# A graph layer with a routed feed-forward layer: a group of 512 nodes in one step or in two

## The chip, the cores and the metric

The kernel runs on one core of one Trainium2 chip. A core has a matrix engine (TensorE, PE in the profile; its weight loads are PEld), a vector engine (VectorE, DVE), a scalar engine (ScalarE, ACT), GpSimd (POOL), a queue engine (SyncE, SP) and 16 DMA engines. Each engine runs its own program; they meet at semaphores. The time is device microseconds (us) of the launch. The kernel before took 2781.99 us, the median of three runs (2778.76 to 2784.24).

## The reference, cut to what matters

```python
# x (12500, 256); 212,500 edges, sorted by dst; all float32
xn  = layernorm(x)
agg = segment_sum(xn[src] * edge_weight[:, None], dst, 12500)
x   = x + agg @ W.T + b
H   = gelu(layernorm(x) @ W1 + b1)               # 12500 x 1024
p   = softmax(H @ Wg + bg); e = argmax(p)        # one of 8 experts for each node
out = x + p[e] * (H @ Wd[e] + bd[e])
```

There is no product over all experts in the kernel: nodes are sorted into lists by their chosen expert and each list is multiplied with its own `Wd[e]`.

## The kernel before, in words

The work has three stages.

*Preamble.* x is normalised and stored as the table `xn_table`; VectorE works out small integer tables from the sorted `dst`, among them `steps_i`, the list of steps.

*Edge stage.* The edges are cut into 104 edge steps of 16 tiles with 128 edges each. For each tile GpSimd issues one indirect DMA (line 403) that gathers 128 rows of `xn_table` into a ring `xring` of three sections, 16 tiles in each; the gathers of step g wait until TensorE is done with step g-3. In `gather_step` TensorE multiplies each tile with a narrow matrix that holds the edge weights (line 515, into `psR`), then runs four matmuls into a bank that nothing reads (line 521), then places the result (line 527); VectorE copies `psR` to `parts` (line 900), adds into `agg` (line 890) and makes the narrow matrix for the next step (lines 847, 857; 857 is the last instruction of an edge step).

The nodes are cut into 25 groups of 512, four blocks of 128 nodes; the last group has 212 real nodes, that is two blocks. As soon as the edges of a group f are all in, a *group step* stands between two edge steps. TensorE and VectorE read its place from `steps_i` and take the same branch. In the group step of f:

- VectorE: `take_sums(f)` copies the sums out of `agg` (929, 930) and clears them; `normalize(f)` waits for the product with W (569), adds x and b and normalises (1003 to 1014). Then come, for the group before, f-1: `rank_choices` (944 to 961), `add_to_lists` (969 to 979) and `second_part`, which copies H to `rows` (1025) and picks the expert (985 to 993; 993 is the last instruction of a group step).
- TensorE: `hidden(f-1)`, that is ranks (548 to 553), eight chunks of H (592) with `messages(f)` (569) after the third, list columns (560), logits (600), transposes of H (614), a fold (621); then the transposes of the normalised group f (578).
- ScalarE: GELU (466), and the copies of the transposed group (461).

So the first group's step has only its own half (`messages(0)`, `transpose_xn2(0)`), and after the loop stands `hidden(24)` by itself, with one more `rank_list` and `extend_list`, since the choices of a group enter the lists one group later.

SyncE stores, for each group, x and the rows of H and logits (row_table, lines 351 and 361), and loads x of the next (356). After the last edge step it loads all `Wd` (379, eight DMAs of 1 MB) and `bd` (381) into the memory where ring and sums were.

*Routed stage.* From the counts of the lists VectorE makes the permutation (lines 1066 to 1093). Then 105 tiles of 128 nodes run: gather rows (420), transpose (648), multiply with `Wd[e]` (658), scale and add, scatter to `out` (428). GpSimd's first gather there waits for the permutation, for `bd`, and for the store of all rows.

Empty places of a tile point to rows behind the real ones, from `PAD_ROW` = 12544 on, one for each of the 128 partitions.

Of the kernel before, what the change touches and what calls it, by code (L numbers as in the profile page):

```python
# [23 lines left out]
P = 128  # L24
# [12 lines left out]
NB = NODES // P  # L37
EDGES = 212500
# [11 lines left out]
STEPS = NG + NF  # L50
# [19 lines left out]
PAD_ROW = N + (-N) % 64  # L70
# [23 lines left out]
def build(nc, x, srcT, dstT, wT, gnn_WT, gnn_b, W1, b1T, Wg, bg, Wd, bd, out):  # L94
    assert PAD_ROW + P <= NODES and NB % LN_ROWS == 0
    ctx = ExitStack()
    with ctx:
# [10 lines left out]
        row_dram = nc.dram_tensor("row_table", (NODES, ROW), F32, kind="Internal").ap()  # L108
# [28 lines left out]
        steps_i = sb("steps_i", [P, STEPS, 6], I32)  # L137
# [65 lines left out]
        u = [selv[:, a * STEPS:(a + 1) * STEPS] for a in range(7)]  # L203
# [118 lines left out]
        def _(sp):  # L322
# [25 lines left out]
            def store_x2(f):  # L348

                sp.wait_ge(s_xn2, f + 1)  # L350
                sp.dma_start(row_dram[bass.ds(f * GROUP, GROUP), 0:C].rearrange("(q p) c -> p q c", p=P),
                             xg[:, :, :]).then_inc(s_x2_st, 16)
                sp.wait_ge(s_x2_st, f * 16 + 16)

            def load_x(f):
                sp.dma_start(xg[:, :, :], x[bass.ds(f * GROUP, GROUP), :]
                             .rearrange("(q p) c -> p q c", p=P)).then_inc(s_xg, 16)

            def store_rows(f):
                sp.wait_ge(s_rows, f + 1)  # L360
                sp.dma_start(row_dram[bass.ds(f * GROUP, GROUP), C:ROW].rearrange("(q p) c -> p q c", p=P),
                             rows[:, :, C:ROW]).then_inc(s_rows_st, 16)
# [19 lines left out]
            store_rows(NF - 1)  # L382
# [65 lines left out]
        def _(act):  # L448
# [9 lines left out]
            def copy_xn2T(f):  # L458
                for k in range(KC):
                    act.wait_ge(s_xt, f * KC + k + 1)  # L460
                    nc.scalar.activation(xn2T[:, k, :], psH[k][:, :], ACT.Identity).then_inc(s_xtc, 1)

            def hidden(f):
                for c in range(HC):
                    act.wait_ge(s_h, f * HC + c + 1)
                    nc.scalar.activation(hidT[:, c, :], psH[c % 2][:, :], ACT.Gelu,  # L466
                                         bias=b1[:, c:c + 1]).then_inc(s_gelu, 1)
                act.wait_ge(s_gp, f + 1)
                nc.scalar.activation(gate_parts[:, :], psG[:, :], ACT.Identity).then_inc(s_gc, 1)

            copy_xn2T(0)
            with act.Fori(0, NF - 1) as f:
                hidden(f)
                copy_xn2T(f + 1)
            hidden(NF - 1)


# [17 lines left out]
        def _(pe):  # L495
# [23 lines left out]

# [23 lines left out]
            def rank_list(b):  # L543
# [4 lines left out]
                nc.tensor.matmul(psE[0][:, at], upper[:, :], oh, start=True, stop=False)  # L548
                for d in range(1, QB):
                    nc.tensor.matmul(psE[0][:, at.start + d * E:at.stop], ones[:, :], oh[:, 0:(QB - d) * E],  # L550
                                     start=False, stop=(d == QB - 1))
                for q in range(QB):
                    mm = nc.tensor.matmul(psE[0][:, total], ones[:, :], oh[:, q * E:(q + 1) * E],
                                          start=(q == 0), stop=(q == QB - 1))
                mm.then_inc(s_rank, 1)

            def extend_list(b):
                pe.wait_ge(s_rank_oh, b + 1)
                for q in range(QB):
                    mm = nc.tensor.matmul(psE[0][:, list_new], slot_oh[:, q, :], col_oh[:, q, :],  # L560
                                          start=(q == 0), stop=(q == QB - 1))
                mm.then_inc(s_list, 1)

            def messages(f):

                pe.wait_ge(s_aggs, f + 1)
                for q in range(QB):
# [6 lines left out]
            def transpose_xn2(f):  # L574
                pe.wait_ge(s_xn2, f + 1)
                for k in range(KC):
                    for q in range(QB):
                        mm = nc.tensor.transpose(psH[k][:, q * P:(q + 1) * P],
                                                 xn2[:, q, k * P:(k + 1) * P], ident[:, :])
                    mm.then_inc(s_xt, 1)  # L580

            def hidden(f, following=None):
                rank_list(f)
                pe.wait_ge(s_xtc, f * KC + KC)
                for c in range(HC):
                    if c == 3 and following is not None:
                        messages(following)
# [3 lines left out]
                    for k in range(KC):  # L591
                        mm = nc.tensor.matmul(psH[c % 2][:, :], w1[:, k, c * P:(c + 1) * P], xn2T[:, k, :],  # L592
# [5 lines left out]
                for c in range(HC):  # L598
                    cg = c % 4
                    mm = nc.tensor.matmul(psG[cg * GATE_COLS:(cg + 1) * GATE_COLS, :], wg[:, c, :], hidT[:, c, :],  # L600
                                          start=(c < 4), stop=(c >= 4))
                mm.then_inc(s_gp, 1)
                if following is not None:

                    pe.wait_ge(s_xn2, f + 2)
                else:

                    pe.wait_ge(s_ev, f * (2 * QB))
                for i in range(2 * QB):
                    half, q = i // QB, i % QB  # L610
# [9 lines left out]
                for q in range(QB):  # L620
# [4 lines left out]
            with pe.Fori(0, STEPS) as k:  # L625
# [11 lines left out]
            hidden(NF - 1)  # L637


            rank_list(NF)  # L640
            extend_list(NF)
# [34 lines left out]
        def _(dve):  # L676
# [94 lines left out]
            for a, span in enumerate((span_tile, span_oct)):  # L771
# [3 lines left out]
            tick(nc.vector.tensor_scalar(stats[:, 0, 0:1], part[:, :], float(GROUP), float(GROUP),  # L775
                                         ALU.mult, ALU.add))
# [400 lines left out]
```

## Time and profile before

| | |
|---|---|
| median of the three runs | 2781.99 us |
| the profiled execution's own time | 2780.53 us |
| its span, first to last instruction | 2778.4 us |
| busy: PE, PEld, DVE, ACT, POOL | 1877.3, 1192.6, 1079.9, 444.4, 1842.4 us |
| mean granted TensorE clock | 0.851 of full speed |

The profile gives each group of instructions with its line, engine, operation, the tile written and the tiles read, the count, the busy time and the mean duration, then the idle time of the engine just before them and what ended it. "issue" means that the engine waited for nothing that the profile shows. In a timeline a row is: start in us, duration in us, engine, line, operation, and in brackets the idle time before it with its releaser. A table by windows has, for each stretch: its length, the busy time of PE, PEld, DVE, ACT and POOL with the instruction counts, the granted clock (1 is 2.4 GHz), the DMA engines' busy share and the GB/s. Spans of POOL are rough. A matmul of 32-bit floats appears as two rows.

### The profile page before, as it was taken

The numbers are of one execution on the slowest core, as the hardware profiler recorded it, in microseconds if no ns is written. First come the engines' busy times: TensorE is split into PE (matmuls) and PEld (weight loads), VectorE is DVE, ScalarE is ACT, GpSimd is POOL, SyncE is SP. The second block draws the span as 40 slices with busy tenths as digits, with TensorE's granted clock in tenths as the row PEclk, the third lists the DMA queues.
The fourth block names the chain that finished last, engine by engine and source line by source line (L and its number), as shares of the span: only waits on it lengthen the run. The fifth ranks groups of instructions, "written<-read, shape, count | busy, mean of one in ns | idle before, by whom it ended". The sixth has DMA issues, their size and how long they took to land.

```text
span 2778.4 us, 39308 instructions
## 1 busy us (share of the span) xinstructions
PE 1877.3 (68%) x10522; PEld 1192.6 (43%) x10523; DVE 1079.9 (39%) x3491; ACT 444.4 (16%) x847; POOL 1842.4 (66%) x1988
## 2 busy tenths in 40 slices
PE   0235675666756667666667566675667777999998
PEld 0122343333433333333334233343333446888887
DVE  8522443334433344343444234443344453333332
ACT  7000110100101001010011000110001113333332
POOL 0677777777777777777777777777777403555553
PEclk9966887888878789788888788887888888999999
DMA  9434444444444444444444344443444354555554
GB/s 396 150 103 119 149 148 120 134 148 147 149 117 132 149 149 148 119 135 147 148 149 149 104 148 149 148 149 111 141 149 149 108 204 152 182 181 179 182 179 128
DMA packets 153598, 420.31 MB, mean 151 GB/s; under 512 B 33320, under 2 KB 67499, under 8 KB 150880
## 3 DMA queue, kind: packets, MB, share of 16 engines
q0 software_dynamic: 100032, 300.27, 36.7%
q1 hardware_dynamic: 53536, 119.73, 11.7%
q14 instruction: 23, 0.19, 0.0%
q8 instruction: 7, 0.11, 0.0%
HBM read 328.02 MB, written 92.82 MB: 151 GB/s over the span
## 4 chain that ended last, share of the span: by engine, by line
POOL 45%; PE 27%; issue 18%; DVE 5%; DMA 2%; DVEq 1%; SPq 0%; POOLq 0%
POOL big L403 45%; PE psA L658 3%; PE psH L658 3%; PE psG L658 3%; PE psE L658 3%; PE psH L592 2%; PE psR L515 2%; PE psA L614 1%; PE psG L600 1%; PE psA L569 1%; DMA src_i<-in_srcT 1%; PE psH L648 1%; PE psE L521 1%; PE psA L648 1%; PE psE L648 1%
## 5 line engine op out<-in xcount | busy, mean ns | idle before, releaser
L403 POOL DMA_INDIRECT big<-xn_table,src_i x1664 | 1610.6, 968 | 581.5 <-issue 579.3
L515 PE MATMUL psR<-big,sel_narrow 128*32 128x256 f32 x3328 | 297.6, 519 | 597.7 <-DMA big<-xn_table,src_i 409.8
L515 PEld LDWEIGHTS psR<-big,sel_narrow 128*32 128x32 f32 x3328 | 127.1, 141 | 715.0 <-issue 630.6
L466 ACT ACTIVATE hidT<-psH,b 128x512 f32<-128x512 f32 x200 | 137.4, 687 | 1506.5 <-PE psH L592 1506.5
L592 PE MATMUL psH<-xn2T,w 128*128 128x512 f32 x800 | 374.4, 624 | 0.0
L900 DVE COPY parts<-psR 128x512 f32<-128x512 f32 x104 | 71.5, 687 | 439.0 <-PE psR L515 438.9
L521 PE MATMUL psE<-w,ident 128*128 128x512 f32 x416 | 240.8, 707 | 0.0
L592 PEld LDWEIGHTS psH<-xn2T,w 128*128 128x128 f32 x800 | 157.8, 200 | 182.6 <-issue 181.3
L894 DVE TENSOR_TENSOR place<-iota,shift_f 128x160 f32<-128x160 f32 x104 | 34.5, 332 | 328.8 <-issue 328.8
L420 POOL DMA_INDIRECT rows<-row_table,stage x105 | 104.1, 991 | 86.8 <-POOL stage L417 86.8
L417 POOL COPY stage<-rel_f 128x1 int32 (+1 forms) x105 | 19.2, 183 | 213.4 <-DVEq L1098 107.2
L1025 DVE COPY rows<-psA 128x512 f32<-128x512 f32 x200 | 128.9, 686 | 40.5 <-PE psA L614 35.9
L527 PEld LDWEIGHTS psE<-place,parts 128*128 128x128 f32 x832 | 107.7, 191 | 84.1 <-DVE parts L900 51.4
L521 PEld LDWEIGHTS psE<-w,ident 128*128 128x128 f32 x416 | 87.0, 234 | 131.8 <-issue 131.8
L890 DVE TENSOR_TENSOR big<-psE,big 128x160 f32 x208 | 67.5, 325 | 185.0 <-PE psE L527 170.2
L428 POOL DMA_INDIRECT out<-big,st_out x105 | 107.3, 1022 | 43.6 <-issue 30.4
L614 PE MATMUL psA<-ident,hidT 128*128 128x128 f32 x800 | 122.6, 287 | 18.4 <-DVE rows L1025 18.4
L527 PE MATMUL psE<-place,parts 128*128 128x80 f32 x832 | 107.1, 272 | 27.6 <-DVE parts L900 27.6
L614 PEld LDWEIGHTS psA<-ident,hidT 128*128 128x128 f32 x800 | 85.3, 142 | 86.9 <-DVE rows L1025 49.7
L560 PE MATMUL psE<-col_oh,big 128*128 128x40 f32 x208 | 38.6, 347 | 95.2 <-DVE big L961 95.2
L658 PE MATMUL psA<-big,hidT 128*128 x432 | 98.7, 382 | 0.0
L569 PE MATMUL psA<-wt,aggs 128*128 128x256 f32 x400 | 92.8, 386 | 6.6 <-DVE aggs L930 6.6
(207 smaller groups left out, 2415.2 us busy)
## 6 DMA issues: line engine op xcount, KB each, us to landing
row_table<-rows SPq DMA_DIRECT2D x25, 2064.0 KB, 8.0
big<-xn_table,src_i POOLq DMA_INDIRECT x1664
big<-in_x SPq DMA_DIRECT2D x10, 1280.0 KB, 17.4
xn_table<-big SPq DMA_DIRECT2D x10, 1280.0 KB, 13.2
big<-in_x SPq DMA_DIRECT2D x25, 512.0 KB
row_table<-big SPq DMA_DIRECT2D x25, 512.0 KB, 3.9
big<-in_Wd SPq DMA_DIRECT2D x8, 1024.0 KB, 12.7
hidT<-in_dstT SPq DMA_DIRECT2D x2, 840.0 KB, 30.5
```

The costliest lines, as they stand in the source:

```text
L403: nc.gpsimd.indirect_dma_start(out=xring[:, h * STEP_TILES + j, :], out_offset=None, in_=xn_dram[:, :], in_offset=bass.IndirectOffsetOnAxi ...
L420: nc.gpsimd.indirect_dma_start(out=grow[i], out_offset=None, in_=row_dram[:, :], in_offset=bass.IndirectOffsetOnAxis(ap=st_in[:, i:i + 1], ...
L428: nc.gpsimd.indirect_dma_start(out=out[:, :], out_offset=bass.IndirectOffsetOnAxis(ap=st_out[:, i:i + 1], axis=0), in_=ybuf[i], in_offset= ...
L466: nc.scalar.activation(hidT[:, c, :], psH[c % 2][:, :], ACT.Gelu, bias=b1[:, c:c + 1]).then_inc(s_gelu, 1)
L515: mm = nc.tensor.matmul(psQ[j * LANES:(j + 1) * LANES, o * C:(o + 1) * C], sel_narrow[:, t, :], xring[:, t, :], start=(odd == 0), stop=(od ...
L521: nc.tensor.matmul(psW[:, :], ident[:, :], w1[:, 0, 0:512], start=True, stop=True)
L527: mm = nc.tensor.matmul(psW[:, at:at + SPAN], parts[:, o, k * P:(k + 1) * P], place[:, o, :], start=True, stop=True)
L569: mm = nc.tensor.matmul(psA[q // 2][:, (q % 2) * C:(q % 2 + 1) * C], aggs[:, k, q * P:(q + 1) * P], wt[:, k, :], start=(k == 0), stop=(k = ...
L592: mm = nc.tensor.matmul(psH[c % 2][:, :], w1[:, k, c * P:(c + 1) * P], xn2T[:, k, :], start=(k == 0), stop=(k == KC - 1))
L614: mm = nc.tensor.transpose(psA[i % 2][:, j * P:(j + 1) * P], hidT[:, 4 * half + j, q * P:(q + 1) * P], ident[:, :])
L658: mm = nc.tensor.matmul(psY2[i], hT2[i][:, c, :], wd[:, bass.ds(e8 + c, 1), :], start=(c == 0), stop=(c == HC - 1))
L1025: nc.vector.tensor_copy(rows[:, q, C + half * 512:C + (half + 1) * 512], psA[i % 2][:, :]).then_inc(s_ev, 1)
```

## The change

The group step is cut in two. The first (kind `SECTIONS`) has `take_sums(f)`, `messages(f)` and `normalize(f)`, and stands where the group step stood. The second (kind `SECTIONS + 1`) has `layers(f)`: transposes, ranks, the chunks of H and all that followed, now for the same group f; it stands one edge step later, or together with the first step of the next group if that comes sooner. The list of steps has 104 + 48 entries; the 25th group is no longer in it, but written out behind the loop for two blocks instead of four. `hidden(24)` for four blocks is gone. Empty places now point to 32 rows from 12500 on, four partitions to a row.

On SyncE the store of the last group's x, which stood ahead of the loads of `Wd` and `bd`, comes behind them.

```diff
-STEPS = NG + NF
+STEPS = NG + 2 * (NF - 1)
+LAST_QB = -(-(N - (NF - 1) * GROUP) // P)          # 2
-PAD_ROW = N + (-N) % 64
+PAD_LANES = 32
...
 @ SyncE
-            store_x2(0)
-            load_x(1)
             with sp.Fori(0, NF - 2) as f:
-                store_x2(f + 1)
-                load_x(f + 2)
+                store_x2(f)
+                load_x(f + 1)
                 store_rows(f)
-            store_x2(NF - 1)
+            store_x2(NF - 2)
+            load_x(NF - 1, LAST_QB)
             store_rows(NF - 2)
...
             sp.dma_start(bd_bc, ...)
-            store_rows(NF - 1)
+            store_x2(NF - 1, LAST_QB)
+            store_rows(NF - 1, LAST_QB)
...
 @ TensorE
-            def transpose_xn2(f):
+            def layers(f, blocks=QB):
+                cols = blocks * P
                 pe.wait_ge(s_xn2, f + 1)
...                                                  # transposes of xn2
-            def hidden(f, following=None):
                 rank_list(f)
                 pe.wait_ge(s_xtc, f * KC + KC)
                 for c in range(HC):
-                    if c == 3 and following is not None:
-                        messages(following)
...
                 mm.then_inc(s_gp, 1)
-                if following is not None:
-                    pe.wait_ge(s_xn2, f + 2)
-                else:
-                    pe.wait_ge(s_ev, f * (2 * QB))
-                for i in range(2 * QB):
+                for i in range(2 * blocks):
...
                 with pe.If(kind == SECTIONS):
-                    before = n.with_bounds(min_val=0, max_val=NF - 2)
-                    hidden(before, before + 1)
-                    transpose_xn2(before + 1)
+                    messages(n.with_bounds(min_val=0, max_val=NF - 2))
                 with pe.If(kind == SECTIONS + 1):
-                    messages(0)
-                    transpose_xn2(0)
-            hidden(NF - 1)
-            rank_list(NF)
-            extend_list(NF)
+                    layers(n.with_bounds(min_val=0, max_val=NF - 2))
+            messages(NF - 1, LAST_QB)
+            layers(NF - 1, LAST_QB)
+            rank_list(NF, LAST_QB)
+            extend_list(NF, LAST_QB)
...
 @ VectorE, the list of steps: partition 2f is the first step of group f, 2f + 1 its second
+            nc.vector.tensor_scalar(second_i, part_i[:, :], 1, None, ALU.bitwise_and)
+            tick(nc.vector.tensor_scalar(group_i, part_i[:, :], 1, None, ALU.logical_shift_right))
...
+            tick(nc.vector.tensor_tensor(second_i, steps_of[:, 0:1], second_i, ALU.add))
+            tick(nc.vector.tensor_tensor(second_i, second_i, steps_of[:, 1:2], ALU.min))
+            tick(nc.vector.tensor_tensor(stats[:, 4, 0:1], second_i, part[:, :], ALU.add))
...
-                with dve.If(kind >= SECTIONS):
+                with dve.If(kind == SECTIONS):
...
                     take_sums(link, f, g, slot, spill)
                     normalize(link, f)
-                with dve.If(kind == SECTIONS):
+                with dve.If(kind == SECTIONS + 1):
...
-                    rank_choices(tie, before)
-                    add_to_lists(tie, before)
-                    second_part(tie, before)
+                    rank_choices(tie, f)
+                    add_to_lists(tie, f)
+                    second_part(tie, f)
...
-            rank_choices(tie, NF - 1)
-            add_to_lists(tie, NF - 1)
-            second_part(tie, NF - 1)
-            rank_choices(tie, NF)
+            take_sums(link, last, NG, last % NS * SLOT, (last - 1) % NS * SLOT + GROUP, LAST_QB)
+            normalize(link, last, LAST_QB)
+            rank_choices(tie, last)
+            add_to_lists(tie, last)
+            second_part(tie, last, LAST_QB)
+            rank_choices(tie, NF, LAST_QB)
             add_to_lists(tie, NF)
```

ScalarE's program follows: for each group the two copies, eight GELUs and one copy of the logits, and two blocks' width for the last.

How the program order moves, as the instructions stand. TensorE, the group step in the loop, before (`psA<-wt,aggs` is `messages`, `psH<-xn2T,w` a chunk of H, `psE<-col_oh,big` the list columns, `psG` the logits, `psA<-ident,hidT` the transposes of H, `psH<-ident,big` those of the normalised group):

```order
L548 MATMUL psE<-chosen,upper 128x32
...
L592 MATMUL psH<-xn2T,w 128x512 x4
L590 ISA
L592 MATMUL psH<-xn2T,w 128x512 x2
L566 REGISTER_ALU
L569 MATMUL psA<-wt,aggs 128x256 x8
...
L560 MATMUL psE<-col_oh,big 128x40 x4
L596 REGISTER_ALU
L600 MATMUL psG<-hidT,wg 32x512 x8
L614 MATMUL psA<-ident,hidT 128x128 x32
L621 MATMUL psE<-fold,big 128x8 x4
L578 MATMUL psH<-ident,big 128x128 x8
```

TensorE, the two group steps in the loop, after the change:

```order
L618 COMPARE_AND_BRANCH
L562 REGISTER_ALU
L565 MATMUL psA<-wt,aggs 128x256 x8
L618 UNCONDITIONAL_BRANCH
L620 COMPARE_AND_BRANCH
L572 REGISTER_ALU
L575 MATMUL psH<-ident,big 128x128 x8
L544 MATMUL psE<-chosen,upper 128x32
...
L557 MATMUL psE<-col_oh,big 128x40 x4
L590 REGISTER_ALU
L594 MATMUL psG<-hidT,wg 32x512 x8
L602 MATMUL psA<-ident,hidT 128x128 x32
```

`messages` has left the chunks of H and stands alone in a branch of its own; the transposes of the normalised group have moved from the end of the step to the start of the second one.

SyncE from the last turn of its loop to the end, before (`row_table<-big` stores x, `row_table<-rows` stores H and logits):

```order
L351 DMA row_table<-big 128x4x256
L361 DMA row_table<-rows 128x4x1032
L379 DMA big<-in_Wd 128x8x256 x8
L381 DMA big<-in_bd 128x2048
L361 DMA row_table<-rows 128x4x1032
```

SyncE from the last turn of its loop to the end, after the change:

```order
L355 DMA row_table<-big 128x4x256
L359 DMA big<-in_x 128x2x256
L363 DMA row_table<-rows 128x4x1032
L379 DMA big<-in_Wd 128x8x256 x8
L381 DMA big<-in_bd 128x2048
L355 DMA row_table<-big 128x2x256
L363 DMA row_table<-rows 128x2x1032
```

Two stores, each of half the width, now stand behind the nine loads where one store of full width stood; the second waits for the first to land.

## Rows read from the trace of the kernel before

**Rows 1.** Table by windows: the end of the edge stage, the routed stage.
```profile
2194.10:2301.30 107.20, 76.90 (x392) 45.67 (x392) 53.06 (x198) 16.92 (x24) 0.00 (x0) 0.85 0.46 155
2301.30:2778.40 477.10, 457.69 (x2520) 408.29 (x2520) 139.99 (x525) 180.36 (x445) 230.52 (x315) 0.98 0.55 172
```

**Rows 2.** Costliest groups and timeline of POOL: all gathers, the first and the last.
```profile
L403 POOL DMA_INDIRECT big<-xn_table,src_i x1664 | 1610.6, 968 | 581.5 <-issue 579.3
...
76.88 1.16 POOL L403 DMA_INDIRECT big<-xn_table,src_i  x1 [74.90 <-issue]
...
2193.12 0.95 POOL L403 DMA_INDIRECT big<-xn_table,src_i  x1 [0.30 <-issue]
```

**Rows 3.** Timeline around one group step, steps 97 to 99; POOL's section 101.
```profile
2074.26 3.64 PE L515 MATMUL psR<-big,sel_narrow 128*32 128x256 f32 x32 [11.62 <-DMA big<-xn_table,src_i]
...
2091.24 3.62 PE L569 MATMUL psA<-wt,aggs 128*128 128x256 f32 x16
...
2119.53 0.19 DVE L993 TENSOR_TENSOR chosen<-route_b,valid 128x32 f32<-128x32 f32 x1
...
2120.98 2.38 PE L515 MATMUL psR<-big,sel_narrow 128*32 128x256 f32 x32 [2.13 <-issue]
...
2132.72 0.95 POOL L403 DMA_INDIRECT big<-xn_table,src_i  x1 [0.30 <-issue]
...
2145.36 0.68 DVE L857 TENSOR_TENSOR sel_narrow<-sel_narrow,w_f  x1
```

**Rows 4.** Timeline of the first group's step, which has no `hidden`.
```profile
182.67 3.64 PE L515 MATMUL psR<-big,sel_narrow 128*32 128x256 f32 x32 [13.70 <-DMA big<-xn_table,src_i]
...
190.36 0.68 DVE L857 TENSOR_TENSOR sel_narrow<-sel_narrow,w_f  x1
194.67 0.72 DVE L929 COPY aggs<-big 128x1024 f32 x1 [3.62 <-issue]
...
196.01 5.98 PE L569 MATMUL psA<-wt,aggs 128*128 128x256 f32 x16 [6.59 <-DVE aggs L930]
...
209.89 1.46 DVE L1014 TENSOR_SCALAR big<-big,meanvar,rstd 128x256 f32<-128x256 f32 x4
...
211.40 1.97 PE L578 MATMUL psH<-ident,big 128*128 128x128 f32 x8 [9.41 <-DVE big L1014]
...
214.02 0.33 DVE L894 TENSOR_TENSOR place<-iota,shift_f 128x160 f32<-128x160 f32 x1 [2.67 <-issue]
```

**Rows 5.** Timeline of `hidden(24)`, which runs alone behind the loop.
```profile
2252.92 0.41 PE L548 MATMUL psE<-chosen,upper 128*128 128x32 f32 x2 [0.93 <-DVE chosen L993]
...
2254.73 15.68 PE L592 MATMUL psH<-xn2T,w 128*128 128x512 f32 x32
...
2281.39 0.19 DVE L993 TENSOR_TENSOR chosen<-route_b,valid 128x32 f32<-128x32 f32 x1
```

**Rows 6.** Timeline: ends of edge steps 101 and 103, start of the routed stage.
```profile
2163.28 0.68 DVE L857 TENSOR_TENSOR sel_narrow<-sel_narrow,w_f  x1
...
2217.46 0.68 DVE L857 TENSOR_TENSOR sel_narrow<-sel_narrow,w_f  x1
...
2301.30 0.18 POOL L417 COPY stage<-rel_f 128x1 int32<-128x1 int32 x1 [107.23 <-DVEq L1098]
```

**Rows 7.** SyncE's timeline at the end of the edge stage; landing times of lines 361, 381.
```profile
2258.26 19.20 SPq L379 DMA_DIRECT2D big<-in_Wd  x8
...
2280.37 0.80 SPq L361 DMA_DIRECT2D row_table<-rows  x1
...
DMA to landing us min/median/max: 6.6/10.2/13.8
...
DMA to landing us min/median/max: 11.5/11.5/11.5
```

**Rows 8.** TensorE's first edge step (timeline); the scan for the list of steps (groups by shape).
```profile
107.64 3.64 PE L515 MATMUL psR<-big,sel_narrow 128*32 128x256 f32 x32 [26.79 <-issue]
...
L778 DVE TENSOR_SCALAR_CACHE_REDUCE rows<-rows,stats 128x1664 f32<-128x1664 f32 x1 | 1.9, 1947 | 0.0
```

More of the change, by code:

```diff
@@ L202, in build @@
         span_tile, span_oct = (xn2T[:, a, 0:NG] for a in range(2))
-        u = [selv[:, a * STEPS:(a + 1) * STEPS] for a in range(7)]
+        u = [selv[:, a * STEPS:(a + 1) * STEPS] for a in range(9)]
         small = xn2T[:, :, :].rearrange("p a b -> p (a b)")
@@ L572, in messages @@
                 mm.then_inc(s_z, 1)
-            def transpose_xn2(f):
+            def layers(f, blocks=QB):
+                cols = blocks * P
                 pe.wait_ge(s_xn2, f + 1)
                 for k in range(KC):
-                    for q in range(QB):
+                    for q in range(blocks):
                         mm = nc.tensor.transpose(psH[k][:, q * P:(q + 1) * P],
@@ L618, in hidden @@
                 pe.wait_ge(s_listed, f + 1)
-                for q in range(QB):
+                for q in range(blocks):
                     mm = nc.tensor.matmul(psE[0][:, q * E:(q + 1) * E], gate_parts[:, q * P:(q + 1) * P],
@@ L817, in _ @@
             is_group, groups, gathers, section, prev = (a.bitcast(I32) for a in (u[2], u[3], u[4], u[5], u[0]))
-            nc.vector.tensor_scalar(prev, groups, float(NS - 1), None, ALU.add)
+            slots, earlier, second, group_of = (u[a].bitcast(I32) for a in (1, 6, 7, 8))
+            nc.vector.tensor_scalar(second, groups, 1, None, ALU.bitwise_and)
+            nc.vector.tensor_scalar(group_of, groups, 1, None, ALU.logical_shift_right)
             tick(nc.vector.tensor_tensor(gathers, iota_i[:, 0:STEPS], groups, ALU.subtract))
+            nc.vector.tensor_scalar(prev, group_of, float(NS - 1), None, ALU.add)
+            nc.vector.tensor_scalar(slots, group_of, NS - 1, None, ALU.bitwise_and)
+            nc.vector.tensor_tensor(second, second, is_group, ALU.mult)
+            nc.vector.tensor_tensor(earlier, gathers, group_of, ALU.subtract)
+            tick(nc.vector.tensor_scalar(section, gathers, 171.0, None, ALU.mult))
             nc.vector.tensor_scalar(prev, prev, NS - 1, None, ALU.bitwise_and)
-            tick(nc.vector.tensor_scalar(section, gathers, 171.0, None, ALU.mult))
+            nc.vector.tensor_tensor(earlier, earlier, is_group, ALU.mult)
             tick(nc.vector.tensor_scalar(section, section, 9, None, ALU.logical_shift_right))
@@ L1016, in normalize, with second_part @@
                 o.then_inc(s_xn2, 1)
-            def second_part(tie, f):
+            def second_part(tie, f, blocks=QB):
                 dve.wait_ge(s_rows_free, f + 1)
                 dve.sem_inc(s_pass_dve, 1)
-                for i in range(2 * QB):
-                    half, q = i // QB, i % QB
+                for i in range(2 * blocks):
+                    half, q = i // blocks, i % blocks
                     dve.wait_ge(s_tr, f * (2 * QB) + i + 1)
```

202 lines of the change are left out of this document (98 added, 104 removed).

## The prediction

> **What bounds the kernel now.** I read the page first: POOL 1842 us busy, PE 1877, neither full, so the stages have different limits. The table by windows cuts it: 107 us lie between the last gather and the first routed one, with POOL at 0.00, and the routed stage of 477 us has PE busy for 458 [rows 1]. Then POOL's groups and timeline: 1664 gathers, 968 ns each, and 581.5 us idle, of which 74.9 stand ahead of the first. That leaves 506.6 over 1663 gaps, 0.30 us each: the gap between any two gathers, so GpSimd never waits for a free section. From 76.88 to 2194.07 (2193.12 + 0.95) it takes 2117.2 us, or 20.36 per edge step [rows 2]. The edge stage is POOL's, and work of TensorE and VectorE in it counts only if it lasts so long that the ring runs full. The chain of waits passes through group steps in the edge stage, but POOL's own rows show no wait there; I go by the rows.
>
> How near is the ring to full? In the step shown, TensorE starts step 97 on its data at 2074.26, and step 98 only at 2120.98, after the group step, 26 us behind its data. It is done at 2123.36; POOL needs that section at 2132.72: 9.4 us to spare [rows 3].
>
> So the change can win at the end of the edge stage, and it can lose by starving POOL.
>
> **The edge stage, part by part.** The first step of a group is in the trace already: the first group's step has only that half. From the end of line 857 (191.04) to the end of line 1014 (211.35) it takes 20.3 us: 3.6 until line 929, then `messages`, which waits for the sums and takes 5.98, then the normalisation [rows 4]. In the usual group step `messages` takes 3.62 [rows 3], under the chunks of H. So this step costs 17.9 to 20.3. I take 20.3: its place in the program is that of rows 4, with TensorE idle for 6.59 ahead of it.
>
> The edge step between the two halves: VectorE is at line 894 2.67 us after the normalisation [rows 4], and TensorE has done its matmuls while VectorE normalised. Three edge steps in a row without data to wait for take 26.3 us (2119.72 to 2146.04), 8.8 each; the matmuls in one of them are 2.38 [rows 3]. I take 2.0 off: 6.8, with 5.9 and 8.8 as ends.
>
> The second half: `hidden(24)` alone took 28.66 from its ranks to the choice (2252.92 to 2281.58) [rows 5]. Ahead of it now come the transposes, 1.97 after a wait [rows 4]. If TensorE enters when line 857 ends, that makes 30.6; TensorE's last part of an edge step ends somewhat before line 857, and with transposes at twice the rate (1.0) and chunks without a slow start (14.0 instead of 15.68) it would be about 27.5. TensorE has waited for VectorE before it, so I take 29.5, nearer to the slow end. The list columns need no normalisation any more and follow H at once, as in `hidden(24)`.
>
> A cycle with four edge steps is then 20.3 + 6.8 + 29.5 + 26.3 = 82.9 us against POOL's 81.4 (4 x 20.36). With five it is 91.7 against 101.8. From the starts of line 929 (25, the first in [rows 4]) 18 intervals have four steps and 5 have five, and at most five fours stand in a row. So the two engines fall behind by 1.5 us per four, 7.5 at worst, and a five clears it. The spare time, from TensorE's start of step s: VectorE ends the step 8.4 later (182.67 to 191.04) [rows 4], then 20.3 + 6.8 + 29.5, and the matmuls of s+2 are done 3.6 after that (2119.72 to 2123.36): 68.6. POOL started section 101 58.5 after TensorE's start of step 97 [rows 3]; it wants the section of s+2 one edge step later in the same count, at 78.8. So 10.2 to spare, more than 7.5: no stall, and the edge stage ends where it did. This is the cover for all that the first half costs, and it is nearly used up.
>
> Unknown here is whether GpSimd's gathers change beside another order of the same VectorE instructions: nothing is added, so I take zero; if a gather took 1% more or less it would be 21 us either way, which I hold unlikely.
>
> The preamble gets some ten small instructions and a second scan of 1.95 us. TensorE's first edge step stood at 107.64 [rows 8]; POOL's first wait for it comes three sections after 76.88, at 138: covered, with 26 us over.
>
> **The end of the edge stage.** Before, line 857 of step 101 ended at 2163.96 and of step 103 at 2218.14; the permutation was out at 2301.30, 83.2 us after it [rows 6]. Between lay a half-hidden group step and `hidden(24)` for four blocks.
>
> After: 2163.96, 4.5 late (three fours), + 20.3 + 6.8 + 29.5 + 8.8 for step 103 = 2233.9, that is 15.8 later than before, since group 23 is now worked off there. Then the last group in two blocks:
> - sums, messages, normalisation: 20.3, less 2.6 for half of `messages` at the slow rate and 2.9 for half of the wide VectorE instructions (lines 929 and 1014 of [rows 4] give 0.3 and 0.7 of that): 14.8.
> - transposes, half of 1.97, and ranks, 2.7: 3.7.
> - the chunks, half of 15.68, and 0.7 for a slow start: 8.5.
> - logits to choice: 11.2 in `hidden(24)` (2270.41 to 2281.58) [rows 5], with half of its eight copies gone: 7.7.
> - from the choice to the permutation 19.7 (2281.58 to 2301.30), less 2.3 for shorter ranks, columns and one-hots: 17.4.
>
> Sum 52.1, so 2286.0 in place of 2301.3: 15.3 us earlier. The routed stage is as it was: the same 105 tiles.
>
> On SyncE the last group's stores stand behind the weights. The weights' loads wait for the sums to be cleared, at about 2239; issuing them took 19.2 and `bd` lands 11.5 after its issue [rows 7], so at about 2270. The x store lands just behind, and the rows of two blocks some 6 later (a full store took 6.6 by itself and 13.8 behind the loads [rows 7]): 2277, before 2286. Nine us of cover; if it went, GpSimd's first routed gather would wait for that store.
>
> TensorE's clock is the price inside these numbers: `messages` took 5.98 after a pause and 3.62 without one, and the stretch at the end of the edge stage shows a granted clock of 0.85 against 0.98 in the routed stage [rows 1, 3, 4]; full is 2.4 GHz, the other level 1.2. The Trainium skill, "TensorE: Matmul & The Clock Gate", section "HAM oscillation — how this bites in real kernels", speaks against this change: a loop whose matmul bursts are parted by waits re-enters the slow rate in each turn, and should be laid out so that they stay together. By that rule, carried to the whole second half, its 14 us of chunks would double. The trace shows only the start slow: 15.68 for 32 rows after a wait. I go by the trace.
>
> **Rivals.**
> 1. *POOL starves.* The cycle is longer than reckoned: a slow second half, or hand-overs I don't see. For: only 1.5 us per four are assumed, and a few us of slow clock in each group are enough. Against: the spare 10.2 and the fives. At 84.5 per four POOL would lose some 5 us and the end come 5 later: near 2776. From 85 on it is slower than before; at 86, 4.6 per four and 7 given back per five make 18 x 4.6 - 5 x 7 = 48, less 10 to spare: 38 lost, 8 more at the end, 15 won: 2782 + 31 = 2813.
> 2. *The stores end last.* The x store waits longer behind 9 MB, and the rows behind it. For: the serial wait is new. Against: nine us of cover. With 8 to 15 us more the gain shrinks to 15 or to 9: 2767 to 2773.
> 3. *Everything runs at the fast rate*, and no lateness builds up: 17.9 and 27.5 instead of 20.3 and 29.5, lateness 0, and 3 less in the last group: 15.3 + 2.4 + 2 + 4.5 + 3 = 27 earlier: 2755.
> 4. *The second half stands right behind the first*, if the list of steps makes it so: then it is 49.8 in one piece, 12 more than before, and the ring runs full in most groups: past 2790. By the diff it can't, save where two groups meet: chance 1 in 100.
>
> **How the numbers follow.** The sum was made on the profiled execution, 2780.5; the median of the runs, 2782, lies 1.5 above. 2782 - 15.3 = 2766.7, so 2766. Chances: forecast 0.60 (2759 to 2774 of its own), rival 1 0.19 (of it 0.12 slower than before by over 0.2%, 0.05 within, 0.02 faster), rival 2 0.08 (0.02 within), rival 3 0.12, rival 4 0.01. A difference of 0.2%, 5.6 us, is about what can be told from none. The forecast leaves 0.04 within that. So faster 0.76, same 0.11, slower 0.13. The range 2752 to 2788 leaves out the far end of rival 1 and little of rival 3.
>
> **What would show it.** Right: POOL's idle in front of line 403 still about 581; `messages` near 6 us; a cycle of 82 to 84; the first routed copy on POOL about 15 earlier, released by VectorE. Wrong: gaps of POOL over 0.4 us released by `psR`, or a first routed gather released by a store.

## The result, and the profile after

The changed kernel took 2793.70 us, the median of seven runs (2791.47 to 2796.10); the kernel before, run beside it, 2785.03 (2778.76 to 2786.32). The ratio is 1.0031, 95% interval 1.0021 to 1.0041: slower by some 9 us, where 2766 was forecast. The profiled execution took 2791.47 us with a span of 2789.5.

I read the page's groups and GpSimd's timeline of after first, to compare with [rows 2]. Columns as there: count, busy, mean ns, idle time; in the timeline start, duration, and in brackets the idle time before.

```profile
L404 POOL DMA_INDIRECT big<-xn_table,src_i x1664 | 1613.6, 970 | 597.1 <-issue 578.3
...
775.54 0.94 POOL L404 DMA_INDIRECT big<-xn_table,src_i  x1 [4.08 <-PE psR L512]
...
1472.87 0.94 POOL L404 DMA_INDIRECT big<-xn_table,src_i  x1 [5.08 <-PE psR L512]
...
1906.31 0.95 POOL L404 DMA_INDIRECT big<-xn_table,src_i  x1 [5.04 <-PE psR L512]
...
2211.72 0.94 POOL L404 DMA_INDIRECT big<-xn_table,src_i  x1 [0.30 <-issue]
...
2311.36 0.18 POOL L418 COPY stage<-rel_f 128x1 int32<-128x1 int32 x1 [98.70 <-DVEq L1093]
```

The idle time is 15.6 us more than the 581.5 before. It sits in five gaps that end with a matmul into `psR`: the three above, and two more of 1.25 and 1.53. GpSimd waited for a free section of the ring. The gathers themselves are busy for 3.0 us more (1613.6 against 1610.6; why is not shown, and in the runs below this sum lies anywhere between 1602.1 and 1616.8), so the last one ends at 2212.7 instead of 2194.1: 18.6 later. The first routed copy is 10.1 later than the 2301.30 of [rows 6], released by VectorE, and the routed stage takes 1.0 longer. These make the 11 us between the profiled executions.

Why the ring ran full is seen in one usual group (timelines of TensorE and VectorE in after; line 846 ends an edge step, as 857 did before):

```profile
1151.56 0.68 DVE L846 TENSOR_TENSOR sel_narrow<-sel_narrow,w_f  x1
...
1156.70 6.18 PE L565 MATMUL psA<-wt,aggs 128*128 128x256 f32 x16 [6.20 <-DVE aggs L919]
...
1170.76 1.45 DVE L1003 TENSOR_SCALAR big<-big,meanvar,rstd 128x256 f32<-128x256 f32 x4
...
1175.88 2.00 PE L523 MATMUL psE<-place,parts 128*128 128x80 f32 x8 [4.89 <-DVE parts L889]
1178.94 0.68 DVE L846 TENSOR_TENSOR sel_narrow<-sel_narrow,w_f  x1
1179.94 1.96 PE L575 MATMUL psH<-ident,big 128*128 128x128 f32 x8 [2.06 <-issue]
1181.69 0.47 PE L544 MATMUL psE<-chosen,upper 128*128 128x32 f32 x2
...
1184.97 15.98 PE L586 MATMUL psH<-xn2T,w 128*128 128x512 f32 x32
...
1212.15 0.19 DVE L982 TENSOR_TENSOR chosen<-route_b,valid 128x32 f32<-128x32 f32 x1
```

The first half goes from 1152.24 to 1172.21: 20.0 us (20.3 forecast). The edge step between takes 7.4, to 1179.62 (6.8). The second half takes 32.7, to 1212.34 (29.5). Over the 24 groups of the loop the second half has a mean of 32.7 (32.3 to 32.9): it is the same everywhere.

The table by windows of the same stretch (length; busy us of PE, PEld, DVE, ACT, POOL with counts; granted clock; DMA share; GB/s) shows the clock:

```profile
1170.00:1174.00 4.00, 0.99 (x3) 0.16 (x1) 2.07 (x8) 0.00 (x0) 3.05 (x4) 1.00 0.38 110
1174.00:1180.00 6.00, 2.06 (x9) 1.85 (x10) 2.77 (x6) 0.00 (x0) 4.51 (x5) 0.61 0.87 274
1180.00:1185.00 5.00, 5.00 (x25) 5.00 (x25) 0.00 (x0) 2.48 (x3) 3.78 (x5) 0.50 0.33 102
1185.00:1201.00 16.00, 16.00 (x36) 7.14 (x36) 2.92 (x15) 4.82 (x8) 12.04 (x14) 0.87 0.35 104
```

TensorE does little from 1170 to 1180 (3.05 us of 10), while VectorE normalises and does its part of the edge step. Its transposes and ranks then take 5.0 us, all of them at a granted clock of 0.50, that is 1.2 GHz, and the chunks begin there too. In `hidden(24)` of before the ranks took 1.8 [rows 5], at 1.00, as its window in the kernel before shows:

```profile
2252.90:2254.73 1.83, 1.81 (x16) 1.81 (x17) 0.00 (x0) 0.00 (x0) 0.00 (x0) 1.00 1.02 408
```

With this the distance from one group's sums to the next (starts of the copy in `take_sums`, 18 intervals with four edge steps) has a mean of 85.2 us (84.2 to 86.4), against 81.6 before, where GpSimd sets it, and 82.9 in the forecast.

At the end of the edge stage (timelines of VectorE and SyncE in after), for [rows 6] and [rows 7]:

```profile
2192.90 0.68 DVE L846 TENSOR_TENSOR sel_narrow<-sel_narrow,w_f  x1
...
2261.25 0.68 DVE L846 TENSOR_TENSOR sel_narrow<-sel_narrow,w_f  x1
...
2263.74 17.81 SPq L379 DMA_DIRECT2D big<-in_Wd  x8
...
2295.20 0.38 SPq L363 DMA_DIRECT2D row_table<-rows  x1
```

Step 101 ends at 2193.6, 25.1 later than the 2168.5 of the forecast; from there to the end of step 103 it takes 68.35 (65.4 forecast); and from that end to the first routed copy 49.4 us, where it was 83.2 before.

### The profile page after: what moved, and what is told of

It is laid out like the page before. It is cut to its first block and busy times, and to the rows that moved or that the text cites. A ratio compares the mean times of both kernels' runs of the same rounds, so it can differ in the third digit from the quotient of the medians.

```text
span 2789.5 us, 39686 instructions
## 1 busy us (share of the span) xinstructions
PE 1942.8 (70%) x10478; PEld 1288.8 (46%) x10479; DVE 1076.4 (39%) x3487; ACT 475.1 (17%) x871; POOL 1845.3 (66%) x1988
## 3 DMA queue, kind: packets, MB, share of 16 engines
q1 hardware_dynamic: 52768, 118.15, 11.7%
## 5 line engine op out<-in xcount | busy, mean ns | idle before, releaser
L404 POOL DMA_INDIRECT big<-xn_table,src_i x1664 | 1613.6, 970 | 597.1 <-issue 578.3
L512 PE MATMUL psR<-big,sel_narrow 128*32 128x256 f32 x3328 | 270.0, 479 | 256.0 <-issue 127.9
L586 PE MATMUL psH<-xn2T,w 128*128 128x512 f32 (+1 forms) x800 | 393.4, 656 | 0.0
L462 ACT ACTIVATE xn2T<-psH 128x512 f32<-128x512 f32 (+1 forms) x50 | 29.4, 588 | 1605.6 <-PE psH L575 1605.6
L523 PE MATMUL psE<-place,parts 128*128 128x80 f32 x832 | 131.5, 310 | 232.9 <-DVE parts L889 232.7
L586 PEld LDWEIGHTS psH<-xn2T,w 128*128 128x128 f32 x800 | 171.8, 219 | 202.9 <-issue 201.2
L523 PEld LDWEIGHTS psE<-place,parts 128*128 128x128 f32 x832 | 124.7, 223 | 299.5 <-DVE parts L889 280.3
L565 PE MATMUL psA<-wt,aggs 128*128 128x256 f32 x392 | 151.0, 567 | 151.1 <-DVE aggs L919 151.1
L517 PE MATMUL psE<-w,ident 128*128 128x512 f32 x416 | 222.5, 659 | 0.0
L565 PEld LDWEIGHTS psA<-wt,aggs 128*128 128x128 f32 x392 | 114.6, 300 | 180.8 <-DVE aggs L919 154.9
L466 ACT ACTIVATE hidT<-psH,b 128x512 f32<-128x512 f32 (+1 forms) x200 | 135.7, 678 | 305.4 <-PE psH L586 305.4
L602 PE MATMUL psA<-ident,hidT 128*128 128x128 f32 x784 | 118.9, 285 | 32.9 <-DVE rows L1014 32.9
```

Source lines behind the costliest of these rows:

```text
L404: nc.gpsimd.indirect_dma_start(out=xring[:, h * STEP_TILES + j, :], out_offset=None, in_=xn_dram[:, :], in_offset=bass.IndirectOffsetOnAxi ...
L466: nc.scalar.activation(hidT[:, c, 0:blocks * P], psH[c % 2][:, 0:blocks * P], ACT.Gelu, bias=b1[:, c:c + 1]).then_inc(s_gelu, 1)
L512: mm = nc.tensor.matmul(psQ[j * LANES:(j + 1) * LANES, o * C:(o + 1) * C], sel_narrow[:, t, :], xring[:, t, :], start=(odd == 0), stop=(od ...
L517: nc.tensor.matmul(psW[:, :], ident[:, :], w1[:, 0, 0:512], start=True, stop=True)
L523: mm = nc.tensor.matmul(psW[:, at:at + SPAN], parts[:, o, k * P:(k + 1) * P], place[:, o, :], start=True, stop=True)
L565: mm = nc.tensor.matmul(psA[q // 2][:, (q % 2) * C:(q % 2 + 1) * C], aggs[:, k, q * P:(q + 1) * P], wt[:, k, :], start=(k == 0), stop=(k = ...
```

## The experiments

Nine kernels were run, each timed beside the kernel before. The theory at the start: the loop loses, because TensorE comes to the second half at the lower clock, the cycle grows past GpSimd's 81.4 us and the ring runs full; the last group wins. The rivals: two blocks are worth little; the place of the second half hurts, and not its length.

| label | edit | median us | ratio to before, 95% |
|---|---|---|---|
| e1_tail_only | loop of before, last group of two blocks | 2768.28 | 0.9947 (0.9934 to 0.9961) |
| e2_last_four | after, last group of four blocks | 2811.30 | 1.0106 (1.0091 to 1.0122) |
| e3_warm | after, 8 matmuls behind `messages` | 2791.89 | 1.0035 (1.0021 to 1.0049) |
| e3b_warm_eleven | the same with 11 | 2790.11 | 1.0009 (0.9999 to 1.0019) |
| e4_two_steps | after, second half two edge steps behind the first | 2765.49 | 0.9940 (0.9926 to 0.9953) |
| e7_two_steps_longer | e4, second half 4.4 us longer | 2857.87 | 1.0246 (1.0228 to 1.0264) |
| e0_right_behind | after, no edge step between | 2885.73 | 1.0361 (1.0343 to 1.0379) |
| e8_shorter_half | after, second half shorter: five of its chunk matmuls are left out | 2757.55 | 0.9916 (0.9901 to 0.9931) |
| e6_two_steps_overlap | e4, group 23 and the last group overlapped | 2754.65 | 0.9881 (0.9864 to 0.9897) |

**The two parts apart.** e1_tail_only keeps the group step of before in the loop:

```diff
-                    messages(n.with_bounds(min_val=0, max_val=NF - 2))
+                    before = n.with_bounds(min_val=0, max_val=NF - 3)
+                    hidden(before, before + 1)
+                    transpose_xn2(before + 1)
...
-            messages(NF - 1, LAST_QB)
-            layers(NF - 1, LAST_QB)
+            hidden(NF - 2, NF - 1, QB, LAST_QB)
+            transpose_xn2(NF - 1, LAST_QB)
+            hidden(NF - 1, None, LAST_QB)
```

> The group steps inside the loop are those of before (one step per group: chunks of H of the group before, with the messages of the next after the third); only the last group is written out behind the loop for two blocks instead of four. My theory: all that the change loses it loses inside the loop, by the cycle of 86 us, and all that it wins it wins in the last group. Then GpSimd shows no gap over 0.4 us, its last gather starts at about 2194 as before, and the permutation is out 10 to 14 us earlier than the 2301.3 of before: 2772 to 2776 against 2785. Rival (the two blocks are worth little, since the chain behind the choice is as long as before): within 4 us of before, 2781 to 2789.

It took 2768.28, 13.3 below the 2781.61 of before beside it, where 9 to 13 were expected. The page and GpSimd's and SyncE's timelines of this kernel:

```profile
L404 POOL DMA_INDIRECT big<-xn_table,src_i x1664 | 1610.6, 968 | 581.6 <-issue 579.5
...
2252.06 18.53 SPq L380 DMA_DIRECT2D big<-in_Wd  x8
...
2273.51 0.80 SPq L363 DMA_DIRECT2D row_table<-rows  x1
...
2284.98 0.18 POOL L418 COPY stage<-rel_f 128x1 int32<-128x1 int32 x1 [90.79 <-SPq L365]
```

No stall, and the permutation out at 2281.3 (end of VectorE's last line, 1106), 20 earlier than the 2301.3 of before. But the copy waits 3.6 us more for the store of rows, which stands behind 9 MB of weights: rival 2 of the prediction, in another kernel than the one that it was meant for. So the two blocks win and the loop loses.

e2_last_four takes the two blocks away:

```diff
-LAST_QB = -(-(N - (NF - 1) * GROUP) // P)
+LAST_QB = QB
```

> After, with the last group written out for four blocks instead of two. My theory: the loop is as in after (stalls of 15 us on GpSimd, last gather at 2212), and only the last group is longer, by half of its chunks (8), half of the eight copies (3.5), half of the wide steps (5) and shorter ranks and columns: 10 to 18 us over after, 2804 to 2812. Rival (the gain came from where the halves stand, not from the two blocks): under 5 us over after.

2811.30, as expected. Its first routed copy starts at 2332.15, 68.2 us after step 103 ended (2263.94); in after it was 49.4. Two blocks in place of four are worth 18.8 us.

**The clock, tried directly.** e3_warm and e3b_warm_eleven:

```diff
                     messages(n.with_bounds(min_val=0, max_val=NF - 2))
+                    for _ in range(8):                       # 11 in the second
+                        nc.tensor.matmul(psW[:, :], ident[:, :], w1[:, 0, 0:512], start=True, stop=True)
```

> After, with eight more matmuls of 128x512 into the bank that nothing reads, behind the messages in the first half of each group, where TensorE waits for the normalisation. My theory: the second half is 32.6 us in place of 29.5 because TensorE comes to the transposes and ranks at the granted clock 0.50; busy through the pause it keeps the upper level, ranks fall from 5.1 to about 2 us, the second half to 28.6 to 30, the cycle from 86 to 82 to 83.5: GpSimd's stalls fall from 15.6 to under 4 us, line 846 of step 103 ends 20 to 30 us earlier, and the time is 2760 to 2775. Rival (the second half is long for what VectorE does in it, the clock is a bystander): ranks get shorter but the cycle stays at 85 to 87, and the time is 2788 to 2800, as in after or longer by the added work.

> As the run with eight added matmuls, but with eleven. Eight left TensorE idle for 2.4 us ahead of the place matmuls, and the transposes and ranks still ran at the granted clock 0.50; eleven last until the place matmuls can start. Theory A (the second half is too long, for its clock): granted clock 1.00 in transposes and ranks, second half 28 to 29 us in place of 32.6, no gap of GpSimd over 0.4 us, the choice of group 23 at about 2231, time 2758 to 2770. Theory B (one edge step between the halves is too little for the ring, whatever the second half takes): ranks get faster, but gaps of GpSimd released by the matmuls of psR stay, 8 us or more in sum, and the time is 2780 or more. If the clock stays at 0.50 the run tells nothing of either.

Both missed: 2791.89 and 2790.11, and GpSimd stalled for 17 and 24 us. They don't speak against the theory, since they didn't do what they were made for. The windows of e3b_warm_eleven in one group:

```profile
649.80:653.60 3.80, 3.80 (x37) 1.82 (x30) 1.52 (x3) 0.00 (x0) 2.89 (x4) 1.00 0.77 226
653.60:658.60 5.00, 2.32 (x14) 2.17 (x13) 1.25 (x3) 0.60 (x1) 3.78 (x5) 0.76 0.68 224
658.60:664.00 5.40, 5.40 (x20) 4.37 (x20) 1.63 (x11) 1.88 (x2) 3.88 (x6) 0.50 0.35 98
```

TensorE works without a pause until 654, at 1.00. Then it pauses for 2.68 us until the branch into the second half has its first transpose, and the clock falls to 0.50 while TensorE is busy again. The pause ahead of the transposes is 2.7 to 3.2 us in all 24 groups; in after it is 1.8 to 2.3. In 18 of the 24 groups the transposes took 2.0 us, as in after; in the other six the slow stretch came a little later, in the chunks (16.6 to 16.9 us). The mean second half is 33.4, no shorter than in after.

**Two edge steps between the halves.**

```diff
+            tick(nc.vector.tensor_scalar(second_i, second_i, 2.0, None, ALU.mult))
             tick(nc.vector.tensor_tensor(second_i, steps_of[:, 0:1], second_i, ALU.add))
```

> After, with the second half two edge steps behind the first in place of one. My theory: what starves GpSimd is first the length of the cycle, which is the same sum of parts here (19.9 + 2 x 7.4 + 32.6 + 2 edge steps), a little shorter or equal, and only then where the two halves stand in it: stalls of 3 to 12 us in place of 15.6, last group's place one edge step closer to the end, so 2784 to 2795. Rival (the ring runs full because two halves stand too close, and the length of the cycle is innocent): no stall at all, last gather at 2195, time 2770 to 2780.

2765.49: my theory's number fell. The rival's "no stall at all" came true, with a time still below its 2770 to 2780. GpSimd's idle time is that of before (page of e4_two_steps), and the first routed copy starts at 2286.11. But the second half itself had changed. Page, timelines of TensorE and VectorE, and then the windows of e4_two_steps:

```profile
L404 POOL DMA_INDIRECT big<-xn_table,src_i x1664 | 1607.2, 966 | 581.5 <-issue 578.5
...
232.91 1.09 PE L575 MATMUL psH<-ident,big 128*128 128x128 f32 x8 [2.32 <-issue]
...
236.36 16.52 PE L586 MATMUL psH<-xn2T,w 128*128 128x512 f32 x32
...
635.46 1.93 PE L512 MATMUL psR<-big,sel_narrow 128*32 128x256 f32 x32
...
652.20 3.64 PE L512 MATMUL psR<-big,sel_narrow 128*32 128x256 f32 x32 [1.68 <-DVE sel_narrow L847]
...
660.60 0.68 DVE L847 TENSOR_TENSOR sel_narrow<-sel_narrow,w_f  x1
660.97 1.09 PE L575 MATMUL psH<-ident,big 128*128 128x128 f32 x8 [1.32 <-issue]
661.90 0.31 PE L544 MATMUL psE<-chosen,upper 128*128 128x32 f32 x2
...
663.60 13.98 PE L586 MATMUL psH<-xn2T,w 128*128 128x512 f32 x32
...
688.85 0.19 DVE L983 TENSOR_TENSOR chosen<-route_b,valid 128x32 f32<-128x32 f32 x1
```

```profile
648.00:652.00 4.00, 1.99 (x8) 1.78 (x8) 2.17 (x5) 0.00 (x0) 2.91 (x4) 0.50 0.83 240
652.00:656.00 4.00, 3.80 (x33) 1.61 (x34) 0.56 (x3) 0.00 (x0) 3.09 (x4) 0.50 0.44 137
656.00:661.00 5.00, 3.68 (x13) 2.02 (x13) 2.17 (x5) 0.00 (x0) 3.78 (x5) 0.81 0.37 105
661.00:664.00 3.00, 3.00 (x25) 2.88 (x26) 0.40 (x2) 2.32 (x3) 2.39 (x3) 1.00 0.32 87
664.00:678.00 14.00, 14.00 (x38) 6.47 (x37) 2.64 (x15) 5.24 (x9) 10.65 (x12) 1.00 0.37 106
```

The same instructions take 27.8 us (661.28 to 689.04) in place of 32.7: transposes and ranks 2.6 instead of 5.0, chunks 14.0 instead of 16.0. The second edge step keeps TensorE busy just ahead of them, it is that step that runs at 0.50, and the transposes start at 1.00. The transposes take 1.1 us in all 24 groups; in 15 the whole second half runs fast (27.1 to 27.8), in nine a slow stretch still falls into ranks and chunks (29.6 to 32.0; the chunks from 236.36 are one); the mean is 28.9. The two sorts differ in the pause of TensorE just ahead of the transposes: 0.8 to 1.4 us in the 15, 1.6 to 2.4 in the nine. That is read from rows; no run sets this pause by itself, and what makes it long or short is not shown.

The distance between groups had not become short everywhere. The 18 intervals with four steps have a mean of 84.8, nearly the 85.2 of after. But the first of the loop and the first behind each interval with five steps take 84.5 to 92.4, since TensorE waits for data there again; of the other twelve eight take 82.1 to 82.5. And those with five steps take 90.3 where after has 93.8: against GpSimd's 101.8 each gives back 11.5 us and not 8.0. So in e4 the lateness (counted from the first group against 20.36 us for each edge step) is gone after every interval with five steps, while in after it has grown to 28 us by the last one with four.

So this run changed place and length at once, and can't decide between them. Three more could.

**Length and place apart.** e7_two_steps_longer keeps the place of e4 and gives the length back; e8_shorter_half keeps the place of after and takes the length away; e0_right_behind goes to the other side.

```diff
 e7
                 rank_list(f)
+                for _ in range(5):
+                    nc.tensor.matmul(psG[:, :], ident[:, :], w1[:, 0, 0:512], start=True, stop=True)
 e8
-                    for k in range(KC):
+                    used = 1 if blocks == QB and c < 5 else KC
+                    for k in range(used):
 e0
+            tick(nc.vector.tensor_scalar(second_i, second_i, 0.0, None, ALU.mult))
```

> As the run with the second half two edge steps behind the first, with five more matmuls of 128x512 behind the ranks in every second half (into the bank of the logits, which is free then): the second half is 32.4 us instead of 28.0, as long as in after, but two edge steps away. Theory A (length): the cycle is 87 to 88 us, lateness piles up over the runs of four-step groups; GpSimd may still stall only 1 to 6 us, since two steps give more room, but the choice of group 23 comes at about 2256 instead of 2234.8, and the time is 2784 to 2796. Theory B (place): no stall, group 23 only some 5 to 9 us later, time 2770 to 2778.

> After, one edge step between the halves as there, but in the 24 groups of the loop the first five of the eight chunks of H multiply only half of the input columns: five matmuls of 128x512 fewer, so H, and with it the choices and the output, are other numbers; the lists and the routed stage have the same number of tiles. Adding eight and eleven matmuls to the first half did not raise the clock in the transposes and ranks, so this takes 4.3 us or more (five at 0.86, more where they ran at the lower level) out of the second half in another way: 32.6 becomes 27 to 28.4, as long as with two edge steps between (28.0), and the place stays. Theory A (length): no gap of GpSimd over 0.4 us, or one or two of under 2, last gather at 2190 to 2196, four-step cycles of 81 to 82.5 us where they were 85.2, time 2755 to 2770. Theory B (place, one edge step is too little): four or more gaps released by psR, 8 us or more in sum, time 2778 or more.

> After, with the second half right behind the first, no edge step between. The cycle has the same parts as in after, less the pause between (some 2 us shorter if anything), but the ring must last through both halves at once, 52 us. If the place of the halves counts as well as the length: GpSimd stalls in most groups, 60 to 90 us in sum, time 2835 to 2870. If only the length of the cycle counts: stalls of 0 to 16 us and a time of 2780 to 2795.

The gathers of the three (page; e7, e8, e0 in this order):

```profile
L404 POOL DMA_INDIRECT big<-xn_table,src_i x1664 | 1609.2, 967 | 652.7 <-issue 575.4
```

```profile
L404 POOL DMA_INDIRECT big<-xn_table,src_i x1664 | 1610.5, 968 | 581.6 <-issue 580.7
```

```profile
L404 POOL DMA_INDIRECT big<-xn_table,src_i x1664 | 1615.1, 971 | 697.3 <-issue 575.5
```

e8: second half 28.7 on the mean, cycle 81.3, no stall, 2757.55. One edge step between the halves is enough if the second half is short, and it got short here with its transposes and ranks still at 5.0 us: it is the length that counts, however it comes about. e7: second half 33.4, cycle 88.3, 15 stalls with 70.7 us in sum, 2857.87. Two steps don't help if it is long. So at either place the length decides whether GpSimd stalls (one step between: 15.6 us at 32.7, none at 28.7; two steps: 70.7 at 33.4, none at 28.9), and the rival, that more room between the halves mends it, is refuted.

The place has a price of its own all the same, and it goes the other way: at nearly the same length e7 has a cycle 3.1 longer than after, and only 0.6 of that lies in the second half. The rest is not taken apart; a likely part of it is the clock of the edge step ahead of the second half: its 32 matmuls into `psR` take 3.2 to 3.6 us in all 24 groups of e4 and e7 (0.50 at 652.20 in e4), and 1.9 in 23 of the 24 of after (1.00 at 635.46 in e4).

My number for e7 was far off (2784 to 2796), though the cycle was put nearly right (87 to 88). I had let the lateness pile up and yet given GpSimd only 1 to 6 us of stalls. 18 x 6.9 late less 5 x 6.5 given back (its intervals with five steps take 95.3) is some 92 us; 70.7 of them came out as stalls.

e0 shows that place counts too, beyond a point: the cycle of 86.5 is not far from that of after, yet it has 23 stalls with 115 us. Both halves in one piece last 53.0 us, so the ring runs full in nearly every group, and even intervals with five edge steps take 107 us, where GpSimd needs 101.8: nothing is made good there. It was slower than I expected (2835 to 2870).

**A version that beats both.** e6_two_steps_overlap takes e4 and writes out the second half of group 23 with the last group's first half inside:

```diff
-            messages(NF - 1, LAST_QB)
+            layers(NF - 2, QB, NF - 1, LAST_QB)      # messages(24) after the third chunk
             layers(NF - 1, LAST_QB)
 @ SyncE: loads of Wd and bd, store of the last x, and only then
+            store_rows(NF - 2)
             store_rows(NF - 1, LAST_QB)
```

> A version that should beat both kernels: the second half two edge steps behind the first; the second half of group 23 is taken out of the loop and holds the sums, messages and normalisation of the last group after its third chunk, as the group step of before did; the store of rows of group 23 comes behind the loads of the weights. The serial first half of the last group (2234.8 to 2246.4) goes beside the chunks: 9 to 12 us less than the run with two steps alone, 2753 to 2757. Rival: the stores of rows, now behind the weights, end last, and GpSimd's first routed copy is released by SyncE: 2760 to 2768.

2754.65, ratio 0.9881, as expected. GpSimd's timeline:

```profile
2273.47 0.19 POOL L418 COPY stage<-rel_f 128x1 int32<-128x1 int32 x1 [80.73 <-DVEq L1101]
```

12.6 us earlier than in e4, and released by VectorE, not by a store: the weights are asked for at 2208.5 here, and the last store behind them has landed at 2258.5.

## Why the prediction was wrong

- *What bounds the kernel* was right: GpSimd's gathers set the edge stage as long as TensorE and VectorE make good in the intervals with five steps what they lose in those with four (e8 and e4, no stall in either).
- *The first half*, 20.3: measured 20.0. Right.
- *The edge step between*, 6.8: measured 7.4, inside the bounds of 5.9 and 8.8.
- *The second half*, 29.5: this is the step that failed. It was put between 27.5 and 30.6, and measured 32.7. The slow end took `hidden(24)` as it stood in [rows 5], with ranks of 1.8 us and only a slow start of the chunks. But there TensorE had waited only 0.93 us for the choice, straight behind a group step, and its ranks ran at 1.00. In after it comes from a first half and an edge step in which it waits for VectorE nearly all the time. The row that showed this price was in my own group: transposes 1.97 after a wait of 9.41 [rows 4]. I had counted that slow rate for the transposes and not carried it through the ranks that follow without a pause (1181.69 to 1184.97, 3.3 us instead of 1.8). Of the 3.2 us, 1.5 lie there and 1.1 in my choice of 29.5 below the slow end; the rest is in small steps.
- *The cycle*, 82.9: measured 85.2. Of the excess of 2.3 the second half gives +3.2, the step between +0.6, and the other three edge steps -1.2 or so (25.1, what is left of 85.2, in place of 26.3), with -0.3 from the first half.
- *No stall*: wrong through the cycle alone. Rival 1 had it: "From 85 on it is slower than before", per four steps. With 85.2 in its arithmetic, 18 x 3.8 less 5 x 7.8 given back less 10 to spare makes 19 us of stalls; 15.6 were measured. The forecast's own arithmetic stood as well: e8, with a second half of 28.7, had no stall and took 2757.55.
- *The last group*, 52.1: measured 49.4. The sum is near, in part by luck: sums, messages and normalisation took 9.7 in place of 14.8 (line 918 copies the sums at 2261.85, without the 3.6 us of idle time ahead of it that the row of the loop has), and all behind them 39.7 in place of 37.3.
- *SyncE's stores*: covered, as forecast: the last one, issued at 2295.20, landed 4.5 us later, 11.7 ahead of the copy. In e1 they were uncovered, since the loads of the weights begin 33.8 us after the end of step 103 there (2218.27 to 2252.06), in after 1.8.
- *The sign*: the last group and what lies behind it are 33.7 us shorter (83.2 to 49.4), and the end of step 103 comes 43.8 later. Of these 43.8 the forecast had 15.8, since group 23 is worked off there. The other 28.0 are lateness at step 101 (25.1) and the longer group of 23 (2.9).

The Trainium skill, "TensorE: Matmul & The Clock Gate", section "HAM oscillation — how this bites in real kernels", was the rule that I weighed and set aside: matmul bursts parted by waits re-enter the slow rate in every turn. The trace agrees that it happens in every group (transposes and ranks at 0.50), and disagrees with the whole-half reading of it (the chunks took 16.0, not 28).

Shown by runs: that the length of the second half decides (e7, e8), that the same instructions take 27.8 where the granted clock is 1.00 through transposes, ranks and chunks (e4), and 32.7 where it is 0.50 in the first two and at the start of the third (after), that the two blocks win 18.8 (e2). Open: whether the clock alone, with one edge step between the halves, would mend it. Two attempts didn't free the second half of its slow stretch.

## What to carry to other kernels

Where a producer with a ring sets the time, write down the cycle of the consumers to the microsecond and compare it with the producer's, and add up what is lost and given back over the whole run: here 3.8 us lost per four steps with 8.0 given back per five ended in stalls, 3.4 with 11.5 given back did not (e4), and the sign of a change of 9 us hung on one term of 32. When a piece of TensorE's work is moved, take its duration from a row with the same pause ahead of it, and follow the clock of that row into what comes next without a pause: here 0.50 lasted through the ranks and into the chunks. An experiment on a suspected cost must first show that it changed that cost: e3 and e3b didn't.

## What was not expected of the hardware

The granted clock answers late, in both directions. In e3b_warm_eleven it fell behind a pause of 2.68 us and stood at 0.50 for 5.4 us in which TensorE was busy throughout; in e4_two_steps it stood at 0.50 from 652 to 656 with TensorE busy for 3.80 of 4.00, and was at 1.00 from 661. So work put ahead of a burst does not by itself keep it at 1.00: in e3b 20 us of it, with a pause of 2.7 to 3.2 us behind, did not, while in e4 one edge step was followed by transposes at 1.00. And the stretch that pays can come some instructions after the pause, as in nine groups of e4 and six of e3b.

A store of 1 MB behind 9 MB of loads took 11.5 us to be seen by GpSimd in e1 (2273.51 to 2284.98). The same store landed 4.5 us after its issue in after, where SyncE waits for the store of x to land before it issues the rows.
